# Recurrent weights split beside the encoding, first input products loaded early, GpSimd's recurrence written out

## The chip, the cores and the metric

The kernel runs on one core of a Trainium2 chip, a single launch. The metric is the device time of that core in microseconds, the median of several runs; lower is better. Engines are named as the profile names them: PE is TensorE, PEld its weight load, DVE VectorE, ACT ScalarE, POOL GpSimd, SP SyncE, whose queue issues all DMAs here.

## What is computed

A small two-layer model over 4 sequences of 512 tokens, width 128: token embedding, causal attention, then four "experts" mixed by a router, a state-space layer and a feature mixer. The change lies in the experts. For each expert (E = 4) and each sequence:

```python
h = _ln(relu(x @ ew1 + eb1) @ ew2 + eb2, eg, ebeta)            # encoding, width D = 256
q, k, v = split(h @ aiw + aib, 3)                              # 16 heads of 16
o = softmax(q @ k.T * SCALE) @ v                               # attention over 512 tokens
h = o @ aow + aob
def step(carry, xt):                                           # an LSTM, forward and backward
    h, c = carry
    zg = xt @ Wi + h @ Wh + b
    i, f, g, o = split(zg, 4)
    c = sigmoid(f) * c + sigmoid(i) * tanh(g)
    h = sigmoid(o) * tanh(c)
hf = _lstm_dir(h, wif, whf, bf); hb = _lstm_dir(h[:, ::-1], wibk, whbk, bbk)[:, ::-1]
```

followed by gates and a decoder over `[hf, hb]`. All in float32; where the kernel multiplies in bf16 it uses the value in three bf16 parts that together hold it.

## The kernel before

The program is a list of phases, one after the other: embed, layer norm, causal attention, layer norm, router, `experts_encode`, `experts_attend`, `recurrence`, `experts_after`, and three more. Each phase has one or two blocks in which every engine runs its own straight list of instructions; a block ends when all engines have reached its end, and after a phase its semaphores are cleared. There is no scheduler: the order on an engine is the order in the code.

**Encoding** goes over 16 blocks (4 experts x 4 sequences). On VectorE a block is: two key adds from PSUM (L798), the last bf16 parts of the block before (L789, two subtractions of 1024 columns, both inputs in SBUF), the norm of the next block (L760 to L775), the value adds (L810), and what the first bf16 part leaves over (L783, again two subtractions in SBUF). TensorE turns the normed tile (L710) once L775 and L810 are through. SP stores q and k parts and the values. GpSimd does nothing here.

**Attention** goes over 16 slabs. Exponentials go to a ring of 8 heads, which lies in the tile `wh` of 64 KB per partition. The input products of the LSTM (x @ Wi + b) are made on TensorE (L1104), kept by VectorE in `zs` (L1188) and stored per slab and direction to `zx` in DRAM (L974). The last slab's products run alone at the end. When the ring is no longer read, SP loads all recurrent weights as float32 into the same tile (L1003).

**Recurrence** has two blocks. The first splits the weights, 8 pieces of 2048 columns, into three bf16 parts each: ScalarE copies (L1387, L1390), VectorE subtracts (L1397, L1400). Beside it GpSimd clears five tiles and sets semaphores, and SP loads the input products of the first 32 steps (two buffers of 16 steps, two directions, L1364). The second block does the 512 steps of four chains (2 directions x 2 pairs of experts). For a step of a chain TensorE does 48 matmuls (L1439), VectorE turns them (L1450), adds pairs and halves (L1457, L1461), and makes the new cell and state (L1467 to L1485); ScalarE does sigmoid and tanh; GpSimd keeps the state (L1528) and places the next step's input products beside the turned ones (L1535). L1457 waits for that placing through `placed`. VectorE and ScalarE are written out over all 512 steps. TensorE loops over 4 steps, and GpSimd loops 8 times over 64 steps:

```python
with pool.Fori(0, S // TURN) as turn:
    for i in range(TURN):
        for x, (way, g) in enumerate(CHAINS):
            pool.wait_ge(tanhed[x], TURN * turn + i + 1)
            keep_state(x, (i - 1) % TURN)
            place_input(x, i)
```

## Time and profile before

| | us |
|---|---|
| median of 3 runs | 5243.91 |
| lowest and highest | 5242.98, 5244.2 |
| the profiled execution | 5246.02 |
| its span, first to last instruction | 5244.2 |
| encoding, about | 290 to 582 |
| attention, about | 584 to 1973 |
| split block | 1973 to 2010 |
| recurrence | 2011 to 4720 |

The trace is one execution. Times in it count from the first instruction. "Idle before" an instruction is put down to the semaphore that came last; "issue" stands for time in which an engine waited for nothing that the profile shows, and PEq or POOLq for an engine's sequencer. A DMA row (SPq) shows its issue, not its transfer; its landing is given apart.

### The profile page before, as it was taken

What the parts mean: (1) busy time and instruction counts of PE and PEld (TensorE: products, weight loads), DVE (VectorE), ACT (ScalarE), POOL (GpSimd) and SP (SyncE); (2) the same over time, 40 slices, a digit from 0 to 9 for tenths busy, and PEclk for the clock granted to TensorE, in tenths of its full rate; (3) what the DMA queues carried; (4) which work ended last, traced back from release to release, by engine and by line L of the source; (5) the groups of instructions that cost most, each with busy time, mean ns of one, the idle gap of its engine ahead of it and who ended that gap; (6) DMA issues with size and microseconds to landing.
All of it is one profiled execution on the core that took longest, in us unless ns stands there. A gap on an engine that the chain in (4) does not pass through costs nothing. (4 is left out here: it accounts for less than half of the span.)

```text
span 5244.2 us, 258310 instructions
## 1 busy us (share of the span) xinstructions
PE 5011.5 (96%) x108704; PEld 3523.4 (67%) x108704; DVE 4117.5 (79%) x19249; ACT 2392.4 (46%) x8343; POOL 1150.5 (22%) x5133
## 2 busy tenths in 40 slices
PE   7989799999999996999999999999999999998995
PEld 4656333333333335999999999899999999984442
DVE  3857666666666648999999999999999999991225
ACT  2734565555555535444444444444444444442332
POOL 0000011111111102333333333333333333330000
PEclk9989899999999998999999999999999999999997
DMA  0034554544545431111111011111111011102210
GB/s 15 1 99 144 135 90 89 112 101 84 126 89 121 91 134 49 37 31 27 41 25 41 17 41 25 41 29 29 41 25 41 17 41 25 41 1 89 72 42 13
DMA packets 378787, 302.27 MB, mean 58 GB/s; under 512 B 146105, under 2 KB 357561, under 8 KB 372954
## 3 DMA queue, kind: packets, MB, share of 16 engines
q1 hardware_dynamic: 378382, 298.20, 23.9%
q14 instruction: 314, 2.57, 0.2%
q8 instruction: 91, 1.49, 0.1%
HBM read 179.14 MB, written 119.01 MB: 57 GB/s over the span
## 5 line engine op out<-in xcount | busy, mean ns | idle before, releaser
L1439 PE MATMUL bank<-lparts,lstate 128*32 128x256 bf16 x98304 | 2697.0, 273 | 55.9 <-PEq L1382 46.8
L1439 PEld LDWEIGHTS bank<-lparts,lstate 128*32 128x32 bf16 x98304 | 2457.4, 97 | 296.1 <-issue 47.6
L1450 DVE STREAM_TRANSPOSE ltz<-bank 128x256 f32<-128x256 f32 x2048 | 920.7, 450 | 9.5 <-PE bank L1439 4.0
L1514 ACT ACTIVATE ltc<-lgc 128x16 f32<-128x16 f32 x2049 | 443.1, 216 | 1030.4 <-DVE lgc L1471 1030.4
L1528 POOL TENSOR_TENSOR wh<-lgate,ltc 128x16 f32<-128x16 f32 x2052 | 471.1, 230 | 1798.6 <-ACT ltc L1514 1727.9
L1255 ACT ACTIVATE wh<-bank 128x512 f32<-128x512 f32 x1024 | 550.0, 600 | 481.9 <-PE bank L1042 481.5
L1167 DVE TENSOR_REDUCE bnegmax<-bank 128x1 f32<-128x512 f32 x1024 | 654.0, 682 | 129.0 <-PE bank L1024 128.5
L1509 ACT ACTIVATE lgate<-lz 128x48 f32<-128x48 f32 x2048 | 498.9, 244 | 521.4 <-DVE lz L1461 521.4
L1535 POOL COPY ltz<-wh 128x64 f32<-128x64 f32 x2048 | 604.1, 295 | 0.0
L1457 DVE TENSOR_TENSOR lhalf<-ltz 128x128 f32<-128x128 f32 x2048 | 581.9, 284 | 10.2 <-POOL ltz L1535 6.1
L1104 PE MATMUL bank<-xT,bw 128*128 128x512 f32 x1024 | 489.4, 602 | 2.7 <-DVE bzs L1188 1.9
L1188 DVE TENSOR_SCALAR bzs<-bank,bcols 128x512 f32<-128x512 f32 x256 | 192.2, 751 | 353.2 <-PE bank L1104 353.2
L1461 DVE TENSOR_TENSOR lz<-lhalf 128x64 f32<-128x64 f32 x2048 | 463.7, 226 | 0.7
L1230 POOL CAST bmaxparts<-bnegmax 128x4 bf16<-128x4 f32 x256 | 49.4, 193 | 1639.9 <-DVE bnegmax L1167 1639.9
L1510 ACT ACTIVATE lgc<-lz 128x16 f32<-128x16 f32 x2048 | 408.1, 199 | 0.0
L1475 DVE TENSOR_TENSOR lstate<-lgate,ltc 128x16 f32<-128x16 f32 x2050 | 407.5, 199 | 0.6 <-PEq L1382 0.3
L1024 PE MATMUL bank<-bkp,bqp 96*128 96x512 bf16 x1024 | 362.4, 388 | 25.0 <-DMA bkp<-qk 24.3
L1471 DVE TENSOR_TENSOR lgc<-lprod 128x16 f32<-128x16 f32 x2049 | 358.5, 175 | 0.0
L1485 DVE TENSOR_TENSOR lstate<-lstate 128x16 f32<-128x16 f32 x2048 | 344.5, 168 | 1.5
L1480 DVE TENSOR_TENSOR lstate<-lstate 128x16 f32<-128x16 f32 x2048 | 338.1, 165 | 0.0
L1104 PEld LDWEIGHTS bank<-xT,bw 128*128 128x128 f32 x1024 | 180.9, 189 | 232.9 <-issue 191.2
L1054 PE MATMUL bank<-wh,bvx 128*17 128x512 f32 x2048 | 313.9, 597 | 0.0
(208 smaller groups left out, 4294.2 us busy)
## 6 DMA issues: line engine op xcount, KB each, us to landing
zx<-bzs SPq DMA_DIRECT2D x32, 2048.0 KB, 7.3
wh<-zx SPq DMA_DIRECT2D x64, 1024.0 KB, 7.4
qk<-eparts SPq DMA_DIRECT2D x96, 256.0 KB, 2.8
bqp<-qk SPq DMA_DIRECT2D x192, 128.0 KB, 4.8
bkp<-qk SPq DMA_DIRECT2D x192, 128.0 KB, 8.1
hs<-wh SPq DMA_DIRECT2D x32, 512.0 KB, 5.8
cmemT<-hs SPq DMA_DIRECT2D x32, 512.0 KB, 4.5
vx<-evx SPq DMA_DIRECT2D x16, 544.0 KB, 4.2
```

Of the source, the lines that this page charges most:

```text
L1104: last = nc.tensor.matmul(product_bank(slab, n)[:], w[:, at:at + P], aT[:, k], start=k == 0, stop=k == KH - 1)
L1167: nc.vector.tensor_reduce(negmax[:, j % NH, qt:qt + 1], bank[qt % 2][:], AX.X, ALU.max, negate=True).then_inc(maxed, 1)
L1255: nc.scalar.activation(pT[:, j % RING, kt], bank[2 + n % 3][:], ACT.Exp).then_inc(exped, 1)
L1439: last = nc.tensor.matmul(bank[x][32 * q:32 * q + 32, 0:256], top[:, x, e, k].rearrange("p m r -> p (m r)"), parts[:, way, g, k, n, e, q], ...
L1450: nc.vector.transpose(tz[:, x].rearrange("p (n w) -> p n w", w=SLOT)[:, :, 0:32], bank[x][:, 0:256].rearrange("p (n c) -> p n c", n=BLOCKS ...
L1457: nc.vector.tensor_tensor(half[:, x], rows[:, 1:3], rows[:, 3:5], ALU.add).then_inc(paired[x], 1)
L1461: nc.vector.tensor_tensor(z[:, x].rearrange("p g u -> p (g u)"), half[:, x, 0].rearrange("p n r -> p (n r)"), half[:, x, 1].rearrange("p n ...
L1509: nc.scalar.activation(gate[:, x], z[:, x, 0:3], ACT.Sigmoid)
L1510: nc.scalar.activation(gc[:, x, 0], z[:, x, 3], ACT.Tanh).then_inc(gated[x], 1)
L1514: nc.scalar.activation(tc[:, x], gc[:, x, 1], ACT.Tanh).then_inc(tanhed[x], 1)
L1528: return nc.gpsimd.tensor_tensor(out.rearrange("p k (e b) -> p k e b", e=2), units(gate[:, x, 2]), units(tc[:, x]), ALU.mult)
L1535: nc.gpsimd.tensor_copy(rows, zx[:, way, i // ZX_STEPS % 2, 8 * g:8 * g + 8, :, at].rearrange("p r n -> p n r")).then_inc(placed[x], 1)
```

## The change

Three things are changed. First, the weights are split by GpSimd during the encoding: SP loads a piece of 1 MB, GpSimd makes the three parts with two copies and two subtractions, and SP stores them (1.5 MB) to a new DRAM tensor `wh_parts`. Piece `i` is stored, and piece `i + 2` loaded, behind the value store of block `2i + 1`. Second, in the attention the ring and the q and k tiles now lie in the tile `parts`, the forward input weights and the tile `o` in `zx_first`, and the backward half of `zs` in `zx_second`. In the last iteration of SP's loop the parts are loaded in three transfers, then the first 16 steps' input products of both directions (the last slab's from SBUF). Only the second buffer is loaded in the recurrence, whose first block is gone; GpSimd's memsets and increments stand at the head of the other. Third, GpSimd's 512 steps are written out.

```diff
 def experts_encode(core, d):
+        wh = core.sb(ctx, "ewh", [P, 2, PIECE])
+        wh_rest = core.sb(ctx, "ewhrest", [P, PIECE])
+        wh_parts = core.sb(ctx, "ewhparts", [P, 2, PARTS, PIECE], BF16)
...
+                def load_piece(i):
+                    sp.dma_start(wh[:, i % 2], d["wh"][:, i * PIECE:(i + 1) * PIECE]).then_inc(wh_in[i % 2], 16)
+
+                def store_piece(i):
+                    sp.wait_ge(wh_part3, i + 1)
+                    sp.dma_start(d["wh_parts"][:, i * PARTS * PIECE:(i + 1) * PARTS * PIECE],
+                                 wh_parts[:, i % 2].rearrange("p n c -> p (n c)")).then_inc(wh_out[i % 2], 16)
+
                 load_expert(0)
                 load_expert(1)
+                for i in range(2):
+                    load_piece(i)
...
+                    if b % 2 == 1:
+                        store_piece(b // 2)
+                        if b // 2 + 2 < PIECES:
+                            load_piece(b // 2 + 2)
                 store_later_parts(steps - 1)
                 for parity in range(2):
+                    sp.wait_ge(wh_out[parity], PIECES // 2 * 16)
...
+            @block.gpsimd
+            def _(pool):
+                for i in range(PIECES):
+                    parts_of = [wh_parts[:, i % 2, n] for n in range(PARTS)]
+                    pool.wait_ge(wh_in[i % 2], 16 * (i // 2 + 1))
+                    if i >= 2:
+                        pool.wait_ge(wh_out[i % 2], 16 * (i // 2))
+                    nc.gpsimd.tensor_copy(parts_of[0], wh[:, i % 2]).then_inc(wh_part1, 1)
+                    pool.wait_ge(wh_part1, i + 1)
+                    if i > 0:
+                        pool.wait_ge(wh_part3, i)
+                    nc.gpsimd.tensor_tensor(wh_rest[:], wh[:, i % 2], parts_of[0], ALU.subtract).then_inc(wh_rested, 1)
+                    pool.wait_ge(wh_rested, i + 1)
+                    nc.gpsimd.tensor_copy(parts_of[1], wh_rest[:]).then_inc(wh_part2, 1)
+                    pool.wait_ge(wh_part2, i + 1)
+                    nc.gpsimd.tensor_tensor(parts_of[2], wh_rest[:], parts_of[1], ALU.subtract).then_inc(wh_part3, 1)
...
 def experts_attend(core, d):
-    core.wh = core.sb(core.lstm, "wh", [P, 2 * E * KH * G4])
+    core.parts = core.sb(core.lstm, "lparts", [P, PIECES * PARTS * PIECE], BF16)
+    core.zx_first = core.sb(core.lstm, "lzxfirst", [P, 2, SLABS, BLOCKS, ZX_STEPS])
+    core.zx_second = core.sb(core.lstm, "lzxsecond", [P, 2, SLABS, BLOCKS, ZX_STEPS])
...
+                def load_first_products(way):
+
+                    chunk = (0, S // ZX_STEPS - 1)[way]
+                    at = chunk * ZX_STEPS * BLOCKS
+                    sp.wait_ge(z_stored[way], 16 * (SLABS - 1))
...
+                def copy_first_products(way):
+                    chunk = (0, S // ZX_STEPS - 1)[way]
+                    sp.wait_ge(z_kept, NH * (SLABS - 1) + BLOCKS * (way + 1))
+                    sp.dma_start(core.zx_first[:, way, SLABS - 1].rearrange("p n t -> p (n t)"),
+                                 zs[way][:, chunk].rearrange("p n t -> p (n t)")).then_inc(zx_first_in, 16)
...
                         if slab == SLABS:
+                            sp.wait_ge(scored_t, BT * NH * SLABS)
+                            load_parts(RING_END, PIECES * PARTS * PIECE)
+                            sp.wait_ge(valued, NH * SLABS - BT)
+                            load_parts(0, RING_END // 2)
                             sp.wait_ge(valued, NH * SLABS)
-                            sp.dma_start(core.wh[:], d["wh"]).then_inc(wh_in, 16)
+                            load_parts(RING_END // 2, RING_END)
+                            sp.wait_ge(o_turned, BT * SLABS)
+                            load_first_products(1)
+                            copy_first_products(0)
+                            load_first_products(0)
...
+                copy_first_products(1)
                 store_products(SLABS - 1, 1)
-                for way in range(2):
-                    sp.wait_ge(z_stored[way], 16 * SLABS)
-                sp.wait_ge(wh_in, 16)
+                sp.wait_ge(z_stored[0], 16 * SLABS)
+                sp.wait_ge(parts_in, 3 * 16)
+                sp.wait_ge(zx_first_in, 2 * (E + 1) * 16)
...
 def recurrence(core, d):
-        with nc.Block() as block:
-            @block.scalar
-            def _(act):
-                for i in range(PIECES + 1):
...
-                for way in range(2):
-                    sp.wait_ge(part3, (way + 1) * PIECES // 4)
-                    for c in range(2):
-                        load_zx(sp, way, c, c)
...
+                for tile in (state, gate, gc, tc, prod):
+                    nc.gpsimd.memset(tile[:], 0.0).then_inc(zeroed, 1)
+                pool.wait_ge(zeroed, 5)
...
-                with pool.Fori(0, S // TURN) as turn:
-                    for i in range(TURN):
-                        for x, (way, g) in enumerate(CHAINS):
...
+                for t in range(S):
+                    for x, (way, g) in enumerate(CHAINS):
+                        if t % ZX_STEPS == 0 and g == 0 and t > 0:
+                            chunk = t // ZX_STEPS
+                            pool.wait_ge(zx_in[way][chunk % 2], 16 * ((chunk + 1) // 2))
+                        if t % HS_STEPS == 1 and g == 0:
+                            pool.wait_ge(hs_out[way][t // HS_STEPS % 2], 16 * (t // TURN) + 1)
+                        pool.wait_ge(tanhed[x], t + 1)
+                        keep_state(x, (t - 1) % TURN)
+                        place_input(x, t)
...
+                sp.wait_ge(core.z_last, 16)
+                for way in range(2):
+                    load_zx(sp, way, 1, 1)
```

On SP's queue, from the last stores of the attention to the recurrence, the program has this order before (`zx` is the products in DRAM, `bzs` the tile they are kept in, `wh` the weights and, in the recurrence, the input buffers):

```order
L956 DMA bkp<-qk 16x8x512 x6
L974 DMA zx<-bzs 128x4096 x3
L1003 DMA wh<-in_wh 128x16384
L974 DMA zx<-bzs 128x4096 x2
L948 UNCONDITIONAL_BRANCH
L77 UNCONDITIONAL_BRANCH
L80 ISA x8
L61 UNCONDITIONAL_BRANCH
L1421 UNCONDITIONAL_BRANCH
L1364 DMA wh<-zx 128x16x128 x4
```

And now:

```order
L1024 DMA zx<-lzxsecond 128x4096
L1028 DMA lparts<-wh_parts 128x16384 x3
L1037 DMA lzxfirst<-zx 128x4x128 x3
L1037 DMA lzxfirst<-zx 128x3x128
L1044 DMA lzxfirst<-bzs 128x128
L1037 DMA lzxfirst<-zx 128x4x128 x3
L1037 DMA lzxfirst<-zx 128x3x128
L1024 DMA zx<-bzs 128x4096
L1044 DMA lzxfirst<-lzxsecond 128x128
L1024 DMA zx<-lzxsecond 128x4096
L998 UNCONDITIONAL_BRANCH
```

The one load has become three, two sets of product loads and two copies follow it ahead of the last slab's stores, and of the four loads behind the block's end two are left (`lzxsecond<-zx`).

On GpSimd's queue the program begins like this before (the first block with work for it is the attention's split of the maxima):

```order
L2114 MEMSET const-uint8-127 128x1
L1222 UNCONDITIONAL_BRANCH
L1230 CAST bmaxparts<-bnegmax 128x4
L1234 ISA
L1234 TENSOR_TENSOR brest<-bnegmax,bmaxparts 128x4
```

And now:

```order
L2156 MEMSET const-uint8-127 128x1
L702 UNCONDITIONAL_BRANCH
L709 CAST ewhparts<-ewh 128x2048
L713 ISA
L713 TENSOR_TENSOR ewhrest<-ewh,ewhparts 128x2048
L715 CAST ewhparts<-ewhrest 128x2048
L717 TENSOR_TENSOR ewhparts<-ewhrest,ewhparts 128x2048
```

The last four of these stand there eight times, in a block that had no GpSimd work. At the head of the recurrence GpSimd's queue reads before:

```order
L1406 MEMSET lprod 128x128
L1382 UNCONDITIONAL_BRANCH
L1522 UNCONDITIONAL_BRANCH
L1538 UNCONDITIONAL_BRANCH
L1538 ISA
L1545 ISA
L1528 TENSOR_TENSOR wh<-lgate,ltc 128x2x8
L1535 COPY ltz<-wh 128x8x8
```

And now:

```order
L1543 UNCONDITIONAL_BRANCH
L1546 MEMSET lstate 128x512
L1546 MEMSET lgate 128x192
L1546 MEMSET lgc 128x128
L1546 MEMSET ltc 128x64
L1546 MEMSET lprod 128x128
L1566 TENSOR_TENSOR lhs<-lgate,ltc 128x2x8
L1573 COPY ltz<-lzxfirst 128x8x8
```

The memsets and the first step stand in one block, and no loop is entered; the last pair of rows is there for each of the 2048 steps of a chain.

## Rows read from the trace of the kernel before

**Rows 1.** the page, busy time of each engine

```profile
PE 5011.5 (96%) x108704; PEld 3523.4 (67%) x108704; DVE 4117.5 (79%) x19249; ACT 2392.4 (46%) x8343; POOL 1150.5 (22%) x5133
```

**Rows 2.** the timeline, attention to recurrence: start us, duration us, engine, line, operation

```profile
1964.85 0.33 SPq L974 DMA_DIRECT2D zx<-bzs  x1
1973.01 0.52 POOL L1406 MEMSET lstate<- 128x512 f32 x1 [72.89 <-POOLq L61]
...
1973.91 0.20 POOL L1406 MEMSET lprod<- 128x128 f32 x1
...
2005.80 4.48 DVE L1400 TENSOR_TENSOR lparts<-wh,lparts 128x2048 bf16<-128x2048 f32 x2
...
2010.84 7.43 PE L1439 MATMUL bank<-lparts,lstate 128*32 128x256 bf16 x176 [46.81 <-PEq L1382]
```

**Rows 3.** VectorE's first subtraction of the split: ns min/median/max

```profile
L1397 DVE TENSOR_TENSOR wh<-wh,lparts x8: 2281/2283/2292, 1975.0 to 2003.6; 128x2048 f32<-128x2048 f32 x8
```

**Rows 4.** two stretches by windows: length; PE, PEld, DVE, ACT, POOL busy; clock, DMA share, GB/s

```profile
2264.70:2349.30 84.60, 84.60 (x3100) 77.11 (x3092) 84.37 (x517) 36.47 (x195) 29.51 (x128) 1.00 0.09 26
2349.30:2433.90 84.60, 83.38 (x3044) 76.17 (x3040) 83.04 (x506) 35.81 (x191) 29.62 (x128) 1.00 0.18 36
```

**Rows 5.** the timeline behind step 64, where GpSimd's loop returns

```profile
2352.30 0.16 DVE L1480 TENSOR_TENSOR lstate<-lstate 128x16 f32<-128x16 f32 x1
...
2353.62 0.29 DVE L1457 TENSOR_TENSOR lhalf<-ltz 128x128 f32<-128x128 f32 x1 [1.03 <-POOL ltz L1535]
...
2354.67 0.32 POOL L1535 COPY ltz<-wh 128x64 f32<-128x64 f32 x1
2354.75 0.28 DVE L1480 TENSOR_TENSOR lstate<-lstate 128x16 f32<-128x16 f32 x1
```

**Rows 6.** waits of the recurrence: us in total, times, longest

```profile
POOL wh L1528 <- issue: 34.0, 7, 5.0
```

**Rows 7.** the timeline, the load of the recurrent weights

```profile
1926.15 0.43 SPq L1003 DMA_DIRECT2D wh<-in_wh  x1
```

**Rows 8.** three other stretches, columns as in rows 4

```profile
1926.20:1950.00 23.80, 20.46 (x64) 10.21 (x65) 7.70 (x15) 2.86 (x5) 0.00 (x0) 1.00 1.05 439
...
1966.00:1970.00 4.00, 0.00 (x0) 0.00 (x0) 0.00 (x0) 0.00 (x0) 0.00 (x0) 0.76 0.94 397
1988.00:1994.00 6.00, 0.00 (x0) 0.00 (x0) 6.00 (x4) 5.21 (x4) 0.00 (x0) 0.50 1.08 292
```

**Rows 9.** the same load, issue to landing

```profile
DMA to landing us min/median/max: 27.7/27.7/27.7
```

**Rows 10.** all of GpSimd's groups: count, busy us, mean ns

```profile
L1535 POOL COPY ltz<-wh 128x64 f32<-128x64 f32 x2048 | 604.1, 295 | 0.0
L1528 POOL TENSOR_TENSOR wh<-lgate,ltc 128x16 f32<-128x16 f32 x2052 | 471.1, 230 | 1798.6 <-ACT ltc L1514 1727.9 <-POOLq L1382 36.7 <-issue 34.0
L1238 POOL TENSOR_TENSOR bmaxparts<-brest,bmaxparts 128x4 bf16<-128x4 f32 x256 | 52.7, 206 | 20.5
...
L1230 POOL CAST bmaxparts<-bnegmax 128x4 bf16<-128x4 f32 x256 | 49.4, 193 | 1639.9 <-DVE bnegmax L1167 1639.9
...
L1406 POOL MEMSET lstate<- 128x512 f32 x1 | 0.5, 524 | 72.9 <-POOLq L61 72.9
```

**Rows 11.** the timeline, one block of the encoding: VectorE, then TensorE

```profile
402.97 2.35 DVE L789 TENSOR_TENSOR eparts<-erest,eparts 128x1024 bf16<-128x1024 f32 x2
...
410.10 1.50 DVE L810 TENSOR_TENSOR evx<-bank,erows 128x512 f32<-128x512 f32 x2
411.52 2.35 DVE L783 TENSOR_TENSOR erest<-eqk,eparts 128x1024 f32<-128x1024 f32 x2
417.12 0.75 DVE L798 TENSOR_SCALAR eqk<-bank,ecols 128x512 f32<-128x512 f32 x1 [3.25 <-PE bank L725]
...
412.43 1.04 PE L710 MATMUL bank<-ident,ehn 128*128 128x128 f32 x8
```

**Rows 12.** the encoding's steady part

```profile
330.00:560.00 230.00, 229.71 (x836) 149.07 (x833) 164.48 (x339) 113.89 (x153) 0.00 (x0) 1.00 0.41 139
```

More of the change, by code:

```diff
@@ L874 @@
 ZX_STEPS = 16
+SLABS = E * B
 def experts_attend(core, d):
@@ L1102, in product @@
                             pe.wait_ge(wi_in[way], 16 * (slab // B + 1))
-                    at = ATT["wi"] + (way * KH + k) * G4 + block * P
-                    last = nc.tensor.matmul(product_bank(slab, n)[:], w[:, at:at + P], aT[:, k], start=k == 0,
+                    at = k * G4 + block * P
+                    last = nc.tensor.matmul(product_bank(slab, n)[:], wi[way][:, at:at + P], aT[:, k], start=k == 0,
                                             stop=k == KH - 1)
@@ L1567, in store_and_load @@
                                 store_hs(sp, way, 2 * turn + c // 2, c // 2)
+                sp.wait_ge(core.z_last, 16)
+                for way in range(2):
+                    load_zx(sp, way, 1, 1)
                 with sp.Fori(0, S // TURN - 1) as turn:
```

115 lines of the change are left out of this document (46 added, 69 removed).

## The prediction

> **What bounds the kernel now.** The page first: TensorE is busy for 5011.5 of 5244.2 us [rows 1], so a gain has to come from a place where it stands still. The timeline at the end of the attention shows the largest one. SP issues the store of the last input products at 1964.85, the five memsets begin at 1973.01, the last two weight subtractions run from 2005.80 to 2010.28, and TensorE's first matmul of the recurrence starts at 2010.84 [rows 2]. From 1973.01 to 2010.84 (37.8 us) ScalarE and VectorE split the recurrent weights and TensorE has nothing to do: 16 VectorE instructions of 2.28 us [rows 3] make 36.5 us of it. The second place is in the recurrence. TensorE issues 3100 matmuls in 84.60 us when undisturbed, but 3044 in the stretch after step 64 [rows 4]. There VectorE waited 1.03 us for GpSimd's copy [rows 5], and GpSimd had stood idle for up to 5.0 us with no releaser, 7 times and 34.0 us in all, once at each return of its loop [rows 6]. Everywhere else I take the work as it is, save the encoding, to which the change adds work.
>
> **The change, part by part.** Sums are made against the profiled span, 5244.2 us; the median of the three runs is 5243.91, so 0.3 us comes off at the end.
>
> *The split block goes, and the loads move.* Removed: the block from 1973.01 to 2010.84, with its four zx loads. What is late next is the DMA queue. SP still reaches the weight load behind the store of slab 14's backward products, at 1926.15 [rows 7]; that store's own wait comes first in the queue, so the earlier waits that the diff names release nothing earlier. From there the queue has to carry: that store, 2.10 MB; the parts, 128 x 49152 x 2 bytes = 12.58 MB in place of 8.39; the first products of 15 slabs for both directions, 2 x 0.98 MB in pieces of 512 bytes; two copies of 0.07 MB; and slab 15's forward store, 2.10 MB. Slab 15's backward store is waited for in the recurrence, 16 steps (84 us) before its data are read: nothing. Rates: from 1926.2 to 1950 the DMAs moved 439 GB/s, and 292 GB/s while zx pieces of 512 bytes came in [rows 8]. So 16.8 MB / 439 = 38.2 us and 2.1 MB / 292 = 7.2 us: the last byte comes at 1926.2 + 45.4 = 1971.6. The queue doesn't run dry on the way: the forward loads and store are issued at about 1951, while the parts run to about 1960, and the copy issued near 1964.9 finds the store still running. From the last store's issue to the memsets 8.2 us went by [rows 2], of which 2.10 MB / 439 = 4.8 us are its bytes and 3.4 us landing, barrier and clearing. A large transfer also has a tail: the weight load was landed 27.7 us after its issue [rows 9], at 1953.9, though nearly all bytes had moved by 1950; I add 1.3 us of that. Memsets at 1971.6 + 3.4 + 1.3 = 1976.3. They ran beside the split and now stand in front: 1.1 us by their rows [rows 2], and 0.7 us for the increments behind them (estimate, 0.3 to 1.5). First matmul at 1978.1 in place of 2010.84: **-32.7 us**. Bounds: nothing faster than the bytes at 439 GB/s with no tail, -36; all 18.9 MB at the 397 GB/s of another stretch [rows 8] with the tail whole, near 1984, -27. TensorE stood still for 46 us before its first matmul and now for 14. That brings no faster clock: it was granted 0.76 from 1966 to 1970 and 0.50 (1.2 GHz) by 1988 [rows 8], so it had begun to fall before the new start.
>
> *GpSimd unrolled.* The seven returns go. The stretches with one hold 44 to 56 matmuls fewer than 3100, 344 in the seven; at 84.60 / 3100 = 27.3 ns each that is **-9.4 us**. At the one end 0, if the straight program stops for its next piece as often; at the other 10, a little more than the row. VectorE and ScalarE run straight programs through the 512 steps and show no such stall, so I stay by the row.
>
> *The split beside the encoding.* GpSimd was idle there and gets 32 instructions over 2048 columns. The trace has only small ones: copies take 193 ns for 4 columns and 295 for 64, subtractions 206 ns for 4 and 230 for 16, a memset 524 for 512 [rows 10]. By slope a subtraction is 0.2 + 2048 x 2.0 to 2.6 ns = 4.3 to 5.5 us; a copy 2.1 us at the memset's 1.0 ns a column, 3.7 at the copies' 1.7. I take 4.5 and, as the small copies read with a stride and these don't, 2.1: 13.2 us for a piece. A piece is due every two blocks, 33 us, so SP doesn't wait for GpSimd in front of the q and k stores, even at the slow ends (18 us). The Trainium skill (GPSIMD Engine Reference, 3.1) gives 4497 ns for such a subtraction against 2293 ns on VectorE; for VectorE this trace has 2283 ns [rows 3].
>
> What it can cost is VectorE's time. The subtraction of L1480 takes 0.16 us while GpSimd is stalled, and 0.28 us where a GpSimd copy had begun 0.08 us before it [rows 5]. I read it as a VectorE instruction with both inputs in SBUF that waits for a GpSimd one. In the encoding four VectorE instructions of each block have such inputs (L789, L783), and the queue behind L789 leads to TensorE: the pair runs 402.97 to 405.32, norm and values' adds follow back to back until 411.60, TensorE takes them up at 412.43 [rows 11]: slack 0.83 us. L783 has 3.25 us until the next key [rows 11]. GpSimd's 13.2 us meet about 0.9 L789 pairs per piece. The mean remainder of an instruction that is running is (2 x 2.1^2 + 2 x 4.5^2) / 13.2 / 2 = 1.9 us; less the slack 1.1, for 8 pieces 8, and with the uneven cases **+10 us**. At the one end 0 (each wait below the slack); at the other +31, where GpSimd's next instruction also gets in between the two of a pair: 8 x 0.9 x (1.9 + 3.3 - 0.83).
>
> The Trainium skill (SBUF — State Buffer, Who interferes with whom) says that such a VectorE instruction and a GpSimd one that reads SBUF exclude each other for a whole instruction, as the 0.28 us suggest; with that rule the sum keeps its +10, without it it would have 0.
>
> *DMA in the encoding.* 2.6 MB more per two blocks are 79 GB/s on top of 139 at a share of 0.41 [rows 12]: hidden. At the end the last piece's 1.57 MB goes ahead of the last four stores: 3.6 us of DMA, most of it before those are ready, **+1.5 us** (0 to 4).
>
> Sum: -32.7 - 9.4 + 10 + 1.5 = -30.6; from the median, 5243.9: **5213.3 us**.
>
> **The rivals.**
> - *No mutual waiting worth speaking of.* The 0.12 us at L1480 are then a cost per instruction. Encoding +0 to 2 in place of 11.5: **5203**. For it: the wait seen is small. Against: so was the GpSimd instruction.
> - *GpSimd gets in between each pair*, the encoding grows by 20 to 31 us: 5223 to 5234, middle **5229**. For it: GpSimd waits while VectorE's first one runs, so it is first in line. Against: VectorE's second comes without a gap [rows 11].
> - *The queue's tail sets the end.* Small pieces and stores mix badly with the long rows and the first matmul comes at 1984: -27 in place of -32.7, **5219**.
> - *The unrolling gives nothing*: straight code stops GpSimd as the loop did: **5223**.
> - *Slower than before.* One mechanism: GpSimd's instructions on 2048 columns cost two or three times what the slopes say (rows with 4 to 64 columns bear on them weakly), each piece fills both its blocks, and every L783 and L789 waits. It decides from (30.6 + 11.5) / 8 = 5.3 us lost per piece; at 7 us, +14: **5258**.
>
> **How the numbers follow.** Forecast 0.5 (5205 to 5222); no waiting 0.17; GpSimd in between 0.17; tail 0.07; unrolling for nothing 0.05; slower 0.04. The range takes the first whole, the second down to 5199 and the third beyond its end: 5199 to 5235. A measurement can tell about 0.2% (10.5 us, so 5233.4) from no change. Faster are the forecast, no waiting, tail, unrolling for nothing, and 0.09 of the third: 0.88. Within 0.2% the rest of the third, 0.08. Slower 0.04.
>
> **What would show it.** Right: 13 to 16 us between the attention's last matmul and the recurrence's first, 46 before; no dips in the matmul count per 16 steps; GpSimd busy for about 105 us in the encoding; L783 or L789 above 1.22 us in some blocks, and TensorE idle behind ehn or evx for 1 to 2 us per piece. Wrong: an encoding that is longer by over 31 us or not at all; a gap in front of the recurrence beyond 20 us, which would be the queue's term; GpSimd idle with no releaser at other steps.

## The result, and the profile after

| | median of the runs | profiled span |
|---|---|---|
| before | 5244.06 us (5242.98 to 5245.98) | 5244.2 us |
| changed | 5281.55 us (5279.41 to 5285.80) | 5277.4 us |
| forecast | 5213.3 us (5199 to 5235) | |

The ratio is 1.0071, 95% interval 1.0058 to 1.0083: the change makes the kernel slower by 0.7%, where 0.6% faster was forecast. The profiled executions, divided at TensorE's first and last matmuls of the attention and of the recurrence, in us:

| stretch | before | changed | difference | forecast |
|---|---|---|---|---|
| up to the attention's first matmul | 598.0 | 669.7 | +71.7 | +11.5 |
| attention, to its last matmul | 1366.0 | 1364.3 | -1.7 | 0 |
| its last matmul to the recurrence's first | 46.8 | 14.7 | -32.1 | -32.7 |
| recurrence, first to last matmul | 2706.1 | 2701.7 | -4.4 | -9.4 |

The rest of the span differs by 0.3 us. So the gain came, 38 us of the 42 that were forecast for the stretches behind the encoding, and the encoding gave back nearly twice as much. The page's row of busy times, to be held against [rows 1]: TensorE's busy time is 11 us longer, and GpSimd has 98 us more.

```profile
PE 5022.5 (95%) x108704; PEld 3531.7 (67%) x108704; DVE 4142.7 (78%) x19233; ACT 2361.6 (45%) x8327; POOL 1248.8 (24%) x5165
```

The timeline of the end of the attention, the counterpart of [rows 2]:

```profile
2005.45 25.55 SPq L1037 DMA_DIRECT2D lzxfirst<-zx  x2
...
2036.23 0.58 SPq L1024 DMA_DIRECT2D zx<-bzs  x1
...
2047.08 0.53 POOL L1546 MEMSET lstate<- 128x512 f32 x1 [76.97 <-POOLq L61]
...
2048.75 3.61 PE L1460 MATMUL bank<-lparts,lstate 128*32 128x256 bf16 x64 [14.74 <-POOLq L1557]
...
2050.08 0.23 POOL L1566 TENSOR_TENSOR lhs<-lgate,ltc 128x16 f32<-128x16 f32 x1 [1.90 <-issue]
...
2061.17 11.14 PE L1460 MATMUL bank<-lparts,lstate 128*32 128x256 bf16 x383 [1.76 <-issue]
```

The last forward store (from bzs) is issued at 2036.23, the memsets begin 10.9 us behind it and the first matmul comes 1.7 us behind their start. TensorE stood still for 14.74 us in place of 46.81. SP had been held up: two issues of the first products, begun at 2005.45, took 25.55 us, so the first copy and the store went out late. The queue's rates over that time, to be held against [rows 8] (columns as there):

```profile
1996.00:2020.00 24.00, 20.48 (x64) 10.21 (x65) 7.70 (x15) 3.05 (x5) 0.00 (x0) 1.00 1.00 414
...
2034.00:2038.00 4.00, 0.02 (x1) 0.00 (x0) 0.75 (x1) 0.00 (x0) 0.00 (x0) 1.00 1.11 284
```

The recurrence, in the stretch of the same length and place as the second of [rows 4], 338.4 us behind the first matmul, and the recurrence's first stretch:

```profile
2387.10:2471.70 84.60, 84.42 (x3091) 76.91 (x3083) 84.05 (x514) 36.38 (x194) 29.80 (x130) 1.00 0.19 38
```

```profile
2048.75:2133.35 84.60, 82.19 (x2892) 73.86 (x2896) 77.73 (x474) 34.43 (x178) 28.43 (x124) 0.98 0.10 27
```

Where there were 3044 matmuls there are 3091, and GpSimd's waits with no releaser [rows 6] have shrunk from 34.0 us in seven to one of 1.9 us at the start. The first stretch has 2892 matmuls, where the kernel before has 2988 in its own: 96 fewer, 2.6 us at 27.3 ns. The largest stop in it is TensorE's 1.76 us at 2061.17, 12.4 us behind its first matmul, with no releaser. Every kernel here that has lost the split block shows such a stop at this place, of 0.7 to 2.0 us, with GpSimd's loop (experiment 7) and without; the kernel before and experiment 1, which keep the block, have none. Its cause stays open.

The encoding is where the change lost. TensorE's groups up to the attention's first matmul: busy us, mean ns of one, then idle us in front of them and their releasers; first of the changed kernel, then of the one before.

```profile
L739 PE MATMUL bank<-ew,eh 128*128 128x256 f32 x256 | 73.3, 439 | 4.2 <-ACT eh L866 4.2
...
L750 PE MATMUL bank<-ident,ehn 128*128 128x128 f32 x128 | 23.5, 338 | 55.0 <-DVE evx L850 46.8 <-DVE ehn L815 8.2
```

```profile
L699 PE MATMUL bank<-ew,eh 128*128 128x256 f32 x256 | 65.1, 400 | 4.5 <-ACT eh L826 4.5
...
L710 PE MATMUL bank<-ident,ehn 128*128 128x128 f32 x128 | 17.0, 275 | 2.5 <-DVE ehn L775 1.8 <-DVE evx L810 0.8
```

In front of the transposes of ehn TensorE was idle for 2.5 us in all, and now for 55.0: 46.8 behind the values' add, 8.2 behind ehn itself. That is +52.5 us. The matmuls that come next also take longer (the transposes 338 ns for 275, the second layer 439 for 400, together +14.7 us; the projections +1.0): the clock that was granted was 1.00 (2.4 GHz) in all of [rows 12], and here it falls behind a stop. The rest is 3.7 us more of waiting for the last q and k, at the very end. One place in full, the timeline of a block with a piece:

```profile
368.57 1.89 POOL L709 CAST ewhparts<-ewh 128x2048 bf16<-128x2048 f32 x1 [32.20 <-DMA ewh<-in_wh]
...
368.92 11.91 DVE L815 TENSOR_SCALAR ehn<-eh,emv,erstd 128x256 f32<-128x256 f32 x4
...
370.54 4.06 POOL L713 TENSOR_TENSOR ewhrest<-ewh,ewhparts 128x2048 f32<-128x2048 f32 x1
...
374.66 1.89 POOL L715 CAST ewhparts<-ewhrest 128x2048 bf16<-128x2048 f32 x1
376.63 4.05 POOL L717 TENSOR_TENSOR ewhparts<-ewhrest,ewhparts 128x2048 bf16<-128x2048 f32 x1
380.76 1.27 DVE L850 TENSOR_TENSOR evx<-bank,erows 128x512 f32<-128x512 f32 x2
...
382.09 1.97 PE L750 MATMUL bank<-ident,ehn 128*128 128x128 f32 x8 [9.38 <-DVE evx L850]
```

The piece lands and GpSimd starts at 368.57, 0.35 us before the norm's four instructions ehn. These take 11.91 us together, where the same four take 1.38 alone, and they end 0.15 us behind GpSimd's last instruction. The values' add, queued behind them on VectorE, comes 10.5 us late, and TensorE, which needs its bank, waits 9.38 us. The windows over the same place, with TensorE's busy time first and the granted clock third from the end:

```profile
366.00:370.00 4.00, 4.00 (x17) 2.88 (x16) 3.66 (x13) 1.50 (x4) 1.43 (x1) 1.00 0.60 225
376.00:380.00 4.00, 0.00 (x0) 0.00 (x0) 4.00 (x2) 0.00 (x0) 3.92 (x2) 0.57 0.00 0
384.00:386.00 2.00, 2.00 (x7) 1.55 (x6) 0.30 (x1) 1.91 (x3) 0.00 (x0) 0.50 0.15 54
386.00:390.00 4.00, 4.00 (x11) 2.18 (x10) 0.75 (x1) 1.43 (x2) 0.00 (x0) 0.90 0.00 0
```

TensorE stood idle, and the clock went to 0.57 and then to 0.50 (1.2 GHz); it was 0.50 still when TensorE had been at work again for 2 to 4 us, and 0.90 in the 4 us behind those. VectorE's groups in the encoding, changed kernel:

```profile
L815 DVE TENSOR_SCALAR ehn<-eh,emv,erstd 128x256 f32<-128x256 f32 x64 | 67.7, 1119 | 0.6
L829 DVE TENSOR_TENSOR eparts<-erest,eparts 128x1024 bf16<-128x1024 f32 x30 | 44.1, 1512 | 0.0
...
L805 DVE BATCH_NORM_STATS2 estats<-eh 128x6 f32<-128x256 f32 x64 | 22.3, 409 | 0.0
...
L810 DVE TENSOR_SCALAR evar<-emv 128x4 f32<-128x4 f32 x16 | 11.2, 698 | 0.5
```

ehn has 1119 ns for 408 before, evar (four columns) 698 for 170, eparts 1512 (30 of its 32 in this window) for 1216. The statistics (L805, 410 ns before) are what they were, though 16 of the 64 begin while a GpSimd instruction runs. The values' add, which has an input in PSUM, is as it was (683 ns for 687), and so is erest (1214 for 1217), but no GpSimd instruction runs when these begin. ehn reads two scalars from SBUF beside its input and evar takes a constant; both are lengthened, so those scalars aren't the reason.

### The profile page after: what moved, and what is told of

It is laid out like the page before. It is cut to its first block and busy times, and to the rows that moved or that the text cites. A ratio compares the mean times of both kernels' runs of the same rounds, so it can differ in the third digit from the quotient of the medians.

```text
span 5277.4 us, 257840 instructions
## 1 busy us (share of the span) xinstructions
PE 5022.5 (95%) x108704; PEld 3531.7 (67%) x108704; DVE 4142.7 (78%) x19233; ACT 2361.6 (45%) x8327; POOL 1248.8 (24%) x5165
## 5 line engine op out<-in xcount | busy, mean ns | idle before, releaser
L1460 PE MATMUL bank<-lparts,lstate 128*32 128x256 bf16 x98304 | 2696.5, 273 | 19.9 <-POOLq L1557 14.7
L1566 POOL TENSOR_TENSOR lhs<-lgate,ltc 128x16 f32<-128x16 f32 x2052 | 471.5, 230 | 1758.3 <-ACT ltc L1535 1756.4
L1334 ACT ACTIVATE lparts<-bank 128x512 f32<-128x512 f32 x1024 | 549.7, 600 | 481.0 <-PE bank L1121 480.9
L1103 PE MATMUL bank<-lparts 96*128 96x512 bf16 x1024 | 360.9, 387 | 29.1 <-DMA lparts<-qk 28.0
L1133 PE MATMUL bank<-lparts,bvx 128*17 128x512 f32 x2048 | 313.9, 597 | 0.0
L1488 DVE TENSOR_TENSOR lprod<-lgate,lgc 128x32 f32<-128x32 f32 x2049 | 308.9, 151 | 0.7 <-ACT lgc L1531 0.7
L1121 PE MATMUL bank<-lparts 99*128 99x512 bf16 x1024 | 307.2, 381 | 0.9 <-ACT lparts L1326 0.6
L1573 POOL COPY ltz<-lzxsecond 128x64 f32<-128x64 f32 x1024 | 301.8, 295 | 0.0
L1103 PEld LDWEIGHTS bank<-lparts 96*128 96x128 bf16 x1024 | 98.3, 97 | 303.3 <-DVE bnegmax L1246 157.3
```

Of the source, the lines that this page charges most:

```text
L1103: nc.tensor.matmul(bank[qt % 2][:], qp[0:KROWS, h, qt * P:(qt + 1) * P], kp[0:KROWS, h], start=True, stop=True).then_inc(scored, 1)
L1334: nc.scalar.activation(pT[:, j % RING, kt], bank[2 + n % 3][:], ACT.Exp).then_inc(exped, 1)
L1460: last = nc.tensor.matmul(bank[x][32 * q:32 * q + 32, 0:256], top[:, x, e, k].rearrange("p m r -> p (m r)"), parts[:, way, g, k, n, e, q], ...
L1566: return nc.gpsimd.tensor_tensor(out.rearrange("p k (e b) -> p k e b", e=2), units(gate[:, x, 2]), units(tc[:, x]), ALU.mult)
```

## The experiments

Every kernel stands beside runs of the kernel before on the same chip; its median there was 5248.7 us in the first four, 5246.0 in the next four and 5245.8 in the last four. Ratios are to these. Where stretches of a trace are given, a few us are scatter: over the eleven traces here with the changed recurrence and GpSimd written out, the recurrence lasts from 2700.3 to 2703.7 us and the attention from 1363.9 to 1367.8.

**1. Unrolling alone.** The kernel before, with GpSimd's recurrence written out:

```
-                with pool.Fori(0, S // TURN) as turn:
-                    for i in range(TURN):
+                for t in range(S):
```

> The kernel before with one part of the change alone: GpSimd's 512 steps written out. The changed kernel's recurrence lasts 2701.4 us from its first to its last matmul against 2705.8 before, and 12 matmuls in each of the seven stretches are lost still. Theory A (the returns cost 7 us, 2.5 us of it given back by a slower start that comes with the early loads): 7 us faster than before, 5237. Theory B (the written-out program gains only the 4.4 us seen): 5239.7. Theory C (my forecast, the whole dip of 9.4 us goes): 5234.5.

5239.4 us, ratio 0.9982 (0.9972 to 0.9992). From its first matmul to its last the recurrence takes 2700.2 us (2706.1 before): -5.9. GpSimd has no wait without a releaser left. The mechanism is as forecast; by the traces a third of the term's 9.4 us isn't there. The medians differ by 9.3 us with an interval of 4 to 15, which can't tell the two sizes apart.

**2. The pieces' instructions on 16 columns.** The changed kernel; loads, stores and waits as they are, GpSimd's 32 instructions short.

```
-                    parts_of = [wh_parts[:, i % 2, n] for n in range(PARTS)]
+                    parts_of = [wh_parts[:, i % 2, n, 0:16] for n in range(PARTS)]
```

> The changed kernel with GpSimd's 32 instructions of the encoding cut to 16 of the 2048 columns (the rest of the recurrent weights is zero, left out of the computation); all DMAs stay. A memset for the unwritten part is added ahead of the encoding, 7 to 10 us. Theory A (VectorE waits for GpSimd's long instructions): the encoding is as long as before, so 5244 - 33.7 - 4.4 + 8 = 5214 (5210 to 5220). Rival B (the added DMA traffic and SP's fuller queue stretch the encoding): the 70 us stay, 5280 or more. Between them: each explains its share.

5218.1 us, ratio 0.9941 (0.9925 to 0.9958); the attention starts at 606.2. With all the DMA traffic of the split and next to none of its GpSimd time, the encoding is 8.2 us longer than before, not 72: 3.4 us of waiting for the first weights (10.8 for 7.4) and 4.8 for the last q and k (29.1 for 24.3). The first of these comes with the clears that this kernel adds ahead of the encoding; the changed kernel, which has none, waits 7.8 us there. The traffic isn't the cause.

**3. Each instruction where there is slack.** The changed kernel with waits in front of GpSimd's four instructions, so that the casts start behind the pair eparts, beside the statistics, and the subtractions behind the pair erest, while VectorE waits for the next key:

```
+                    pool.wait_ge(*((normed, BT) if i == 0 else (part3[0], 2 * i - 1)))
                     nc.gpsimd.tensor_copy(parts_of[0], wh[:, i % 2]).then_inc(wh_part1, 1)
...
+                    if i > 0:
+                        pool.wait_ge(rested[0], 2 * i)
                     nc.gpsimd.tensor_tensor(wh_rest[:], wh[:, i % 2], parts_of[0], ALU.subtract)
...
+                    if i > 0:
+                        pool.wait_ge(part3[0], 2 * i)
...
+                    pool.wait_ge(rested[0], 2 * i + 1)
```

> The changed kernel with waits on VectorE's semaphores in front of GpSimd's 32 instructions: a copy begins when VectorE's last part of a block is made (then it adds from PSUM and takes statistics for 3.5 us), a subtraction when the rest of the block is made (then it waits for TensorE and adds keys, 5.6 us). The work is the same. Theory A (each waiting VectorE instruction waits for one GpSimd instruction that it meets): nearly none meets one, encoding +0 to 8 us against before, total 5206 to 5214. Rival B (DMA traffic, or GpSimd's busy time as such): the encoding stays 70 us longer, 5275.

5215.1 us, ratio 0.9935 (0.9918 to 0.9952), attention from 603.5. The timeline of one block, GpSimd's and VectorE's instructions:

```profile
403.04 2.35 DVE L835 TENSOR_TENSOR eparts<-erest,eparts 128x1024 bf16<-128x1024 f32 x2
...
405.55 1.89 POOL L710 CAST ewhparts<-ewh 128x2048 bf16<-128x2048 f32 x1 [3.92 <-DVE eparts L835]
...
408.87 1.38 DVE L821 TENSOR_SCALAR ehn<-eh,emv,erstd 128x256 f32<-128x256 f32 x4
...
411.59 2.35 DVE L829 TENSOR_TENSOR erest<-eqk,eparts 128x1024 f32<-128x1024 f32 x2
...
414.45 4.08 POOL L716 TENSOR_TENSOR ewhrest<-ewh,ewhparts 128x2048 f32<-128x2048 f32 x1 [7.02 <-DVE erest L829]
```

The same work on the same engines, with the same number of bytes, and ehn takes its 1.38 us again. What cost the change 66 us was only when GpSimd's instructions run.

**4. Four instructions of 512 columns for each of 2048.** The changed kernel, the same arithmetic:

```
+                    for c in range(4):
+                        n, at = 4 * i + c, slice(512 * c, 512 * (c + 1))
```

> The changed kernel with each of GpSimd's instructions cut into four of 512 columns, done in the order copy, subtract, copy, subtract for each quarter. Same work, some 10% more GpSimd time. Theory A (a VectorE instruction waits for the one GpSimd instruction that runs, then gets its turn): the four instructions of the norm wait for about 1 us each, 3 to 5 us a piece in place of 12; encoding +15 to 35 us against before, total 5222 to 5242. Rival B (GpSimd keeps the port until its chain is through): 12 us a piece as now, 5277 or more.

5231.1 us, ratio 0.9967 (0.9954 to 0.9980), attention from 616.9: with a quarter of the length per instruction (611 and 1157 ns) ehn has 683 ns in the mean. Here the other instructions are met as well. erest beside a piece:

```profile
418.41 0.61 POOL L711 CAST ewhparts<-ewh 128x512 bf16<-128x512 f32 x1
418.49 3.70 DVE L825 TENSOR_TENSOR erest<-eqk,eparts 128x1024 f32<-128x1024 f32 x2
...
419.10 2.02 POOL L715 TENSOR_TENSOR ewhrest<-ewh,ewhparts 128x512 f32<-128x512 f32 x1
```

Taken singly the two erest run from 418.49 for 1.60 us and from 420.02 for 2.17. The first ends 1.07 us behind the cast that ran when it came, GpSimd's subtraction takes 2.02 us where it takes 1.16 alone (it waits for VectorE), and the second erest ends 1.07 us behind that one. So the waiting goes both ways, in turns. Theory A had 5222 to 5242 us.

**5 and 6. Only the casts long, only the subtractions long.** The changed kernel with the other two instructions of a piece on 16 columns.

> The changed kernel with GpSimd's two casts of each piece on all 2048 columns, as in the change, and its two subtractions on 16 columns, so that the third part is zero beyond these (part of the computation left out). Tiles that are read where nothing wrote them are cleared ahead of the encoding. Theory A: a VectorE instruction of the norm that comes while a GpSimd instruction runs ends when that one ends, so its time is that of the one instruction. A piece is then a chain of 1.9, 0.2, 1.9 and 0.2 us; the four instructions of the norm that write ehn take about 4.5 us where they meet it (11.9 in the change, 1.4 alone), the longest single one about 2 us (4.2 in the change); less the slack of 0.8 us that is 2.3 us a piece: the attention's first matmul near 620 (607 with 16 columns throughout, 669.7 in the change), 5230 us. Rival B: a wait costs the same whatever runs on GpSimd (an arbitration per instruction): ehn still 11.9 us for the four, first matmul near 665, 5275. Rival C: only the subtractions with two inputs hold VectorE off: as with 16 columns, first matmul at 607, 5218.

> The other half of the same experiment: GpSimd's two subtractions on 2048 columns, its two casts on 16 (the parts are then wrong beyond these; part of the computation left out). Theory A: a piece is a chain of 0.2, 4.06, 0.2 and 4.06 us; the longest ehn is 4.2 us as in the change, the four take 8 to 9 us where they meet it, less 1.4 and the slack some 6 us a piece: the attention's first matmul near 650, 5260 us. Rival B: 5275 as above. Rival C: the subtractions alone make the whole loss, and the casts none: the same 5275, with casts alone at 5218.

Casts: 5227.5 us, ratio 0.9966 (0.9953 to 0.9978), attention from 614.4. Subtractions: 5257.4 us, ratio 1.0019 (1.0010 to 1.0029), attention from 642.8. One place of the first, then one of the second:

```profile
364.05 4.05 DVE L821 TENSOR_SCALAR ehn<-eh,emv,erstd 128x256 f32<-128x256 f32 x4
...
365.74 1.89 POOL L721 CAST ewhparts<-ewhrest 128x2048 bf16<-128x2048 f32 x1
```

```profile
368.29 4.07 POOL L719 TENSOR_TENSOR ewhrest<-ewh,ewhparts 128x2048 f32<-128x2048 f32 x1
...
368.55 8.68 DVE L821 TENSOR_SCALAR ehn<-eh,emv,erstd 128x256 f32<-128x256 f32 x4
...
372.70 4.05 POOL L723 TENSOR_TENSOR ewhparts<-ewhrest,ewhparts 128x2048 bf16<-128x2048 f32 x1
```

The four ehn take 4.05 us beside the long casts, 8.68 beside the long subtractions, 11.91 beside both. TensorE's waits behind the values' add go the same way: 0.8 us in all with 16 columns, 6.7 with the casts, 27.1 with the subtractions, 46.8 in the change. A wait lasts until the GpSimd instruction that it meets has ended. A cost per instruction (rival B) would have given both kernels the same time, and rival C falls with the 6.7 us of the casts. The totals say less than these rows: both kernels carry the clears ahead of the encoding, 5 us of waiting for the first weights (13.0 and 12.9 us for 7.8 in the change), and at 614.4 the casts lie below the 620 that theory A gave.

**7. Experiment 3 with GpSimd's loop back.**

> The changed kernel with GpSimd's instructions in the encoding each let start right behind a VectorE instruction with slack behind it (e3_timed, 5215.1 us), and GpSimd's recurrence in its loop of 64 steps again, as before the change. What the loop costs on top of e3_timed is the unrolling's term. Theory A: 4.4 to 5.9 us (the recurrence of the change lost 4.4 us, the unrolling alone 5.9): 5219.5 to 5221, with seven dips of 44 to 56 matmuls. Rival B: the whole 9.4 us of the prediction, hidden in the change by something else that it brings: 5224.5. Rival C: with the rest of the change there, the unrolling is worth nothing: 5215.

5219.3 us, ratio 0.9948 (0.9932 to 0.9965). The recurrence takes 2707.9 us from first matmul to last, 2701.7 in experiment 3: the loop costs 6.2 us there, and its seven waits are back:

```profile
POOL lhs L1572 <- issue: 33.9, 7, 5.0
```

The unrolling was thus worth 5.9 us alone and 6.2 here. The 4.4 us of the changed kernel are its worth less the slower first steps. With the scatter of 3.4 us in such stretches the three can't be told apart.

**8. Experiment 3 with the last piece's store first.** Its store goes out ahead of the last block's q and k stores and no longer in front of the final ones:

```
+                    if b == steps - 1:
+                        store_piece(PIECES - 1)
...
-                    if b % 2 == 1:
+                    if b % 2 == 1 and b < steps - 1:
```

> e3_timed, with the store of the last piece's parts issued ahead of the last block's stores of q and k in place of behind them. In e3_timed the attention's first matmul comes at 604.1, 4.6 us behind the kernel before with its GpSimd unrolled (599.5), though TensorE's work ends at the same time: SP issues 1.57 MB at 575.68, in front of the last four stores. Theory A: those bytes are on the path; 8.7 us earlier they are hidden: first matmul at 599 to 600.5, 5210 to 5211.5 us. Rival B: the queue carries all of it in the end and the last q and k stores wait as long: 604, 5215. Rival C: the bytes in front of the last block's first stores hold up ScalarE's next parts: later than 605.

5207.0 us, ratio 0.9929 (0.9912 to 0.9946), attention from 597.1: the lowest median of this study, though its interval overlaps that of experiment 3. TensorE's wait for q at the attention's start, the largest row of its waits there (us, times, longest), of experiment 3 and of this one:

```profile
PE bank L1109 <- DMA lparts<-qk: 29.7, 1, 29.7
```

```profile
PE bank L1111 <- DMA lparts<-qk: 24.9, 1, 24.9
```

The 29.7 and 24.9 us differ by 4.8, as theory A has it; the kernel before has 24.3. Experiment 7, which stores as experiment 3 does, had 28.6, so about 1 us of the 4.8 may be scatter. Theory A had the first matmul at 599 to 600.5 and 5210 to 5211.5 us; that it came lower on both isn't explained. Each against the kernel before on its own chip, experiment 3 gains 33.6 us and this one 39.0, which are 5.4 apart.

**9. The norm on ScalarE.** The changed kernel; ehn is made by ScalarE, after VectorE has made the negative product enmr on four columns.

```
+                    nc.vector.scalar_tensor_tensor(nmr[:], mv[:, :, 0], -1.0, rstd[:], ALU.mult, ALU.mult)
...
+                        nc.scalar.activation(hn[:, b % 2, t], h2[:, b % 2, t], ACT.Identity, scale=rstd[:, t:t + 1],
+                                             bias=nmr[:, t:t + 1]).then_inc(normed, 1)
```

> The changed kernel with the norm's four instructions that write ehn on ScalarE (x times rstd plus the negative of mean times rstd) in place of VectorE; VectorE makes the negative product on four columns. GpSimd's pieces run when they are ready, as in the change. Theory A: the serial waits of ehn go, but VectorE's other instructions with SBUF alone behind them meet the piece in their place: the small product waits for one GpSimd instruction, erest and eparts pairs for one each: some 3 us a piece in place of 9: the attention's first matmul at 620 to 640 (669.7 in the change), 5230 to 5250 us. Rival B: ScalarE waits for GpSimd as well: ehn on ScalarE up to 4 us each, first matmul beyond 660, 5270 or more. Rival C: with ehn gone nothing is left to wait: 605, 5216.

5277.5 us, ratio 1.0059 (1.0042 to 1.0076), attention from 666.6, which looks like rival B and isn't. ScalarE's four ehn take 2.08 us together beside a running piece, 589 ns in the mean with one or without. VectorE's small product enmr took 3.7 us in the three places where it met one, and 0.16 elsewhere. TensorE's waits show where the time went:

```profile
PE bank L741 <- ACT eh L867: 32.7, 16, 4.9
...
PE bank L752 <- DVE evx L851: 12.9, 8, 4.4
```

Behind evx there are 12.9 us in place of 46.8, but the first layer's output eh, which ScalarE now makes behind the norm in its queue, is waited for 16 times, once in each block, 32.7 us in all: a cost of the order that I gave ScalarE, with or without a piece. The run tells that ScalarE doesn't wait for GpSimd; as a remedy it was badly built. Theory A's 5230 to 5250 us was missed, and the total says nothing on its sum.

**10. ehn in the form that also sums.** The changed kernel, VectorE's instruction with a sum written out:

```
-                                                ALU.subtract, ALU.mult).then_inc(normed, 1)
+                                                ALU.subtract, ALU.mult, accum_out=hsum[:, t:t + 1]).then_inc(normed, 1)
```

> The changed kernel with the norm's four instructions in the form that also writes out its sum (a small tile that nothing reads; with that form the second operation may be taken for the sum, so that the values can be off: part of the computation may be changed). Theory A: it is the form of the instruction that decides whether VectorE and GpSimd exclude each other; the accumulating one uses one port and doesn't wait: four ehn together under 2.5 us beside a piece, what is left are the waits of the pairs erest and eparts: first matmul of the attention 615 to 640, 5225 to 5250 us. Rival B: every single-input instruction from SBUF to SBUF that isn't a statistics one waits: ehn 11.9 us for the four as in the change, 670, 5277 to 5282.

5241.6 us, ratio 0.9989 (0.9979 to 0.9999), attention from 632.0. Beside a piece:

```profile
360.19 1.89 POOL L710 CAST ewhparts<-ewh 128x2048 bf16<-128x2048 f32 x1 [21.83 <-DMA ewh<-in_wh]
...
361.50 0.54 DVE L816 TENSOR_SCALAR_CACHE_REDUCE ehn<-eh,emv,erstd 128x256 f32<-128x256 f32 x1
...
362.16 4.09 POOL L714 TENSOR_TENSOR ewhrest<-ewh,ewhparts 128x2048 f32<-128x2048 f32 x1
...
363.16 6.99 DVE L824 TENSOR_TENSOR erest<-eqk,eparts 128x1024 f32<-128x1024 f32 x2
```

Each ehn takes 0.54 us beside the cast, whatever runs (19 of the 64 begin beside a running GpSimd instruction, and none is longer); in their place the two erest wait (6.99 us, singly 4.16 and 2.90). With the same input, scalars and columns it is the form of the VectorE instruction that decides. The Trainium skill (SBUF — State Buffer, Who interferes with whom) says so: copies, casts and tensor_scalar between SBUF tiles may take the pair of ports that GpSimd uses, the form that writes its accumulator may not. The trace agrees, with 0.54 us against up to 4.2.

**11. GpSimd only writes.** Memsets of the same tiles in place of the four instructions.

> The changed kernel with GpSimd's four instructions of each piece replaced by memsets of the same tiles, so that GpSimd writes and doesn't read (the parts are zero; the split is left out). Theory A: a VectorE instruction with two SBUF inputs waits only for a GpSimd instruction that reads, one of the tensor_scalar kind for any: ehn above 1 us each where it meets a memset of 1 to 2 us, erest and eparts at 1.22 us throughout: first matmul of the attention 610 to 640. Rival B: memsets hold off both kinds: eparts or erest above 1.5 us where they meet one. Rival C: without reads on GpSimd nothing waits: ehn 0.41 us, 603 to 607, 5215 to 5218 us.

5243.1 us, ratio 0.9997 (0.9987 to 1.0007), attention from 630.2. First a block where the memsets meet ehn, then one where they meet eparts:

```profile
359.36 1.81 POOL L709 MEMSET ewhparts<- 128x2048 bf16 x1 [30.98 <-DMA ewh<-in_wh]
...
359.82 7.16 DVE L815 TENSOR_SCALAR ehn<-eh,emv,erstd 128x256 f32<-128x256 f32 x4
```

```profile
408.70 1.80 POOL L713 MEMSET ewhrest<- 128x2048 f32 x1
...
409.63 2.35 DVE L829 TENSOR_TENSOR eparts<-erest,eparts 128x1024 bf16<-128x1024 f32 x2
...
410.56 1.80 POOL L715 MEMSET ewhparts<- 128x2048 bf16 x1
```

The four ehn take 7.16 us, one memset of 1.8 us each; the pair eparts takes its own 2.35 us beside two of them, and no eparts or erest of this kernel is longer. So there are two rules, as theory A has it: a tensor_scalar from SBUF to SBUF waited for every kind of GpSimd instruction that was tried, casts, subtractions and memsets, one with two SBUF inputs only for those that read.

**12. One wait per piece.** The changed kernel with the four instructions back to back behind an even block's norm:

```
+                    pool.wait_ge(normed, BT * (2 * i + 1))
```

> The changed kernel with one wait at the head of each piece: its four GpSimd instructions then run back to back behind the norm of an even block, so that ehn never meets them, and the pairs erest and eparts always do. Theory A (each VectorE instruction from SBUF waits for one GpSimd instruction, and GpSimd's next for it): by the durations seen, the second erest ends 4 us late, hidden by the 3.25 us ahead of the next key but for 1, the second eparts 4.3 us late; less the slack of 0.8 that is 3.5 to 4.5 us a piece, 28 to 36 in all on top of e3_timed's 603.5: first matmul of the attention at 631 to 640, 5243 to 5251 us, GpSimd's instructions 0.87 us longer behind each pair. Rival B: only the norm's series of four costs anything; the pairs hide: 603 to 608, 5215 to 5220 us.

5251.2 us, ratio 1.0010 (1.0000 to 1.0019), attention from 638.6: both at the upper end of what theory A gave from the durations seen before. One pair of each kind:

```profile
420.09 6.81 DVE L824 TENSOR_TENSOR erest<-eqk,eparts 128x1024 f32<-128x1024 f32 x2
...
428.15 6.59 DVE L830 TENSOR_TENSOR eparts<-erest,eparts 128x1024 bf16<-128x1024 f32 x2
```

erest takes 6.81 us where 2.35 is its own, eparts 6.59. ehn is at 408 ns throughout. With the two rules and the durations known, such a placement could be priced ahead of its run.

## Why the prediction was wrong, point by point

- *The split block goes* (-32.7): right, -32.1 measured, and the gap is 14.7 us as foretold (13 to 16). Inside the sum one thing went otherwise: I had the forward store issued 13 us ahead of the attention's last matmul (1951 against 1964.0), and it went out 2.2 us behind it, since SP was held up for 25.55 us in the issues of the first products. By then the parts had landed (at 2033.6), and only product loads were still landing, until 2040.1; the store landed 8.7 us behind its issue, where the one before took 6.3, and the end was nearly the same.
- *GpSimd unrolled* (-9.4): the mechanism right, the size not. The 344 missing matmuls were counted against 3100 per stretch; with the loop gone such a stretch still has about 12 fewer, so some 260 come back, 7.1 us by that count and 5.9 to 6.2 by the spans of experiments 1 and 7. The changed kernel loses 2.6 us in its slower first steps, of which the sum had nothing.
- *GpSimd's durations*: right. 32 instructions take 98.9 us (forecast 105); the subtraction 4.06 us alone (4.5), the cast 1.89 (2.1). The 4497 ns that I cited from the Trainium skill (GPSIMD Engine Reference, 3.1) are for an addition in float32 throughout; the second operand here is bf16, and the trace's 4.06 us decide.
- *The split beside the encoding* (+10, to +31 at most; 66 of the 71.7 us fall here): this is the step that failed, in two places. First, "four VectorE instructions of each block have such inputs (L789, L783)" took the rule that [rows 5] suggested, two inputs in SBUF, for the only one. The norm's tensor_scalar instructions, four ehn (L775) and evar (L770), have one tensor as input, and wait for more kinds of GpSimd instructions, not fewer (experiments 10 and 11). The page that I cited for the first rule (the Trainium skill, SBUF — State Buffer, Who interferes with whom) has the second one in the next lines. Second, the price. "The mean remainder of an instruction that is running", 1.9 us, holds for one VectorE instruction that comes alone. Four in a row each wait for one GpSimd instruction: GpSimd starts its next 0.06 to 0.08 us behind its last, and the next ehn meets that one. At worst, in two of the blocks, the wait is then the piece's whole chain, 11.9 us, and the upper bound for a pair (1.9 + 3.3) shows that I had the mechanism in hand and not the series.
- *How often a piece meets them*: I took 0.9 meetings per piece, as if its time were random. It isn't. SP asks for the next piece behind the stores at a block's end, and it lands 9.6 to 9.9 us later in four cases and 13.4 to 14.2 in the other two. With the first two pieces, loaded ahead, five of the eight began just before or at the norm and met two to four of its ehn (at 312, 369, 452, 536 and 581); the other three met evar or the pair eparts. A chance place was here one that the program sets, and a bad one.
- *The clock*: left out. TensorE's matmuls take 15.7 us more, of the 71.7. They take it behind the seven stops of 5 to 9 us (the first piece's four waits counted as one): the transposes have 425 to 428 ns in the six blocks with a stop in front of them and 375 in the first, against 272 to 280 in the other nine, and in the 4 us behind each of the six stops the granted clock was 0.50 (1.2 GHz), in one of them 0.65. Of TensorE's time before a recurrence I had asked this question, of the encoding not.
- *DMA in the encoding* (+1.5): 3.7 us in the changed kernel, 5.4 in experiment 3, near 0 in experiment 8. The four q and k stores waited behind the piece's 1.57 MB, as I had said; that "most of it" would be gone before was wrong, since SP issued it at the same moment as the four.
- *The rivals*: the slower case had the right stretch and the wrong cause. It wanted GpSimd's instructions to be two or three times as long; they were as forecast, and the loss per piece was 9 us all the same (it decided from 5.3). At a chance of 0.04 it was priced as if only duration could bring it about. Rival 2, GpSimd between each pair, is what the trace shows at both pairs that are met (the eparts at 424 and at 507); its end of +31 was too low because it counted neither ehn nor evar.

## What to carry to other kernels

Before work is given to an idle GpSimd beside VectorE, list the VectorE instructions of that stretch by form and operands. Here a tensor_scalar from SBUF to SBUF waited for any GpSimd instruction, one with two SBUF inputs for any that reads. Statistics (0.41 us), the reciprocal (0.18), the form that also sums (0.54) and instructions with an input in PSUM (0.68 to 0.75) took the same time with a GpSimd instruction running as without. And n that wait in a row waited for n GpSimd instructions, up to the four of a piece; price the longest such row, not the mean remainder. Then place each long GpSimd instruction by a semaphore where VectorE's next instructions are of the other kinds or where it waits anyway: here this alone turned +0.7% into -0.65%, and with the last store out of the way -0.7%.

## What the runs showed of the hardware that I had not expected

- A VectorE instruction on four columns (evar, 0.17 us alone) took up to 3.94 us beside GpSimd. Its size is no protection.
- ehn takes 408 ns for 256 columns, no less than the statistics' 409 on the same columns. So its time gives no hint that it waits for GpSimd; only its form does. The Trainium skill (VectorE: DVE Perf Modes, The perf-mode tier table) has fp32 tensor_scalar in SBUF at twice the rate of one element per cycle; at 256 columns with its two scalars read from SBUF, no run here shows that.
- The instruction that waits is recorded as running: a row's duration holds the wait, and the "idle before" columns show nothing. On VectorE the loss is to be looked for in mean ns against the same line of the kernel before.
- GpSimd's own delay by VectorE is small: 0.87 us for each pair instruction it meets (a subtraction 4.93 for 4.06, a cast 2.77 for 1.89), and none to be seen by ehn (beside the four at 369 its casts take 1.89 us and its subtractions 4.06 and 4.05).
